# Scan stage of a recurrent mixer: which engine rounds two operands to their high parts, and in what order three engines and the matmul queue take their steps

## The reference, cut to what matters

```python
proj = jnp.einsum('bsd,od->bso', h, in_proj_w)
hBC = jax.nn.silu(causal_conv(hBC, conv_w, conv_b))
# hid: 128 heads x 64, B and C: 8 groups x 128, dt = softplus(...), A_full = A * dt
M = jnp.einsum('bcihn,bcjhn->bcijh', Ch, Bh) * jnp.transpose(L, (0, 2, 3, 4, 1))
Y_diag = jnp.einsum('bcijh,bcjhp->bcihp', M, hc)
decay_states = jnp.exp(A_cs[..., -1:] - A_cs)
states = jnp.einsum('bclhn,bhcl,bclhp->bchpn', Bh, decay_states, hc)
...
Y_off = jnp.einsum('bclhn,bchpn,bhcl->bclhp', Ch, prev_states, jnp.exp(A_cs))
yg = y * jax.nn.silu(gate)
ygr = ygr * jax.lax.rsqrt(jnp.mean(ygr * ygr, axis=-1, keepdims=True) + EPS)
out = jnp.einsum('bsd,od->bso', y, out_proj_w)
```

## Time and profile before

| | before |
|---|---|
| median of 3 runs | 1997.73 us |
| the profiled execution | 2001.5 us |
| its span, first to last instruction | 1999.6 us |
| PE busy | 1926.9 us (96%) |
| PEld busy | 1548.9 us (77%) |
| ACT busy | 1609.5 us (80%) |
| DVE busy | 1540.3 us (77%) |
| POOL busy | 1523.4 us (76%) |
| mean granted TensorE clock | 0.996 |

### The profile page before, as it was taken

The page is one execution under the profiler, slowest core; times in us unless marked ns, Lnnn a source line. Parts: engine busy times, 40 slices in busy tenths (PEclk is TensorE's granted clock), DMA queues, the critical chain, the costliest instruction groups (busy, mean ns, idle before and its releaser), DMA issues.

```text
span 1999.6 us, 32828 instructions
## 1 busy us (share of the span) xinstructions
PE 1926.9 (96%) x10675; PEld 1548.9 (77%) x10675; DVE 1540.3 (77%) x2806; ACT 1609.5 (80%) x3244; POOL 1523.4 (76%) x1114
## 2 busy tenths in 40 slices
PE   8999999999999999999999999999999999999998
PEld 6574667777888888888888878787878888888876
DVE  8787898866777777777777777777777878787878
ACT  5354866657898989898989898989888888888886
POOL 5644778647787878787878787878787787878887
PEclk9999999999999999999999999999999999999999
DMA  5625323543333333434333343434343434343333
GB/s 203 195 68 140 100 89 110 163 166 116 119 106 122 103 122 104 127 99 126 110 115 120 106 126 100 134 101 130 104 124 104 130 100 126 109 153 117 118 107 122
DMA packets 114474, 241.74 MB, mean 121 GB/s; under 512 B 23681, under 2 KB 24706, under 8 KB 113794
## 3 DMA queue, kind: packets, MB, share of 16 engines
q1 hardware_dynamic: 110466, 227.06, 36.7%
q0 software_dynamic: 3840, 12.59, 2.2%
HBM read 226.75 MB, written 12.85 MB: 120 GB/s over the span
## 4 chain that ended last, share of the span: by engine, by line
PE 28%; ACT 20%; DVE 13%; POOL 11%; issue 7%; DMA 1%; SPq 0%; ACTq 0%; DVEq 0%; POOLq 0%
PE ps L75 7%; PE ps L76 6%; PE ps L77 6%; POOL w_lo L2710 6%; ACT s_lm L2214 5%; PE ps L2129 4%; DVE s_cv L2457 3%; ACT s_scale L2237 3%; ACT s_cv L2247 2%; ACT s_hid L2281 2%; PE ps L2137 2%; POOL s_y_lo L2741 2%; DVE xs L2502 2%; POOL s_ssq L2720 2%; DVE s_hdt L2445 2%
## 5 line engine op out<-in xcount | busy, mean ns | idle before, releaser
L75 PE MATMUL ps<-h_hi,w_hi 128*128 128x512 f32 x1168 | 471.7, 404 | 13.5 <-POOL w_lo L2710 8.6
L2710 POOL TENSOR_TENSOR w_lo<-w_raw,w_hi 128x1024 fp32r<-128x1024 f32 x142 | 337.8, 2387 | 186.5 <-ACT w_hi L2197 186.5
L2457 DVE SCALAR_TENSOR_TENSOR s_cv<-ps,s_par,s_cv 128x511 f32<-128x511 f32 (+2 forms) x480 | 359.1, 748 | 128.3 <-ACT s_cv L2247 117.1
L76 PE MATMUL ps<-h_lo,w_hi 128*128 128x512 f32 x1168 | 456.0, 390 | 0.0
L77 PE MATMUL ps<-h_hi,w_lo 128*128 128x512 f32 x1152 | 450.9, 391 | 0.0
L2214 ACT ACTIVATE s_lm<-s_rows,s_steps 128x128 f32<-128x128 f32 x1024 | 324.0, 389 | 24.6 <-PE ps L2129 24.6
L2736 POOL TENSOR_TENSOR s_lm<-s_lm,s_cbt 128x512 f32<-128x512 f32 x256 | 327.8, 1307 | 14.4 <-ACT s_lm L2229 11.9
L75 PEld LDWEIGHTS ps<-h_hi,w_hi 128*128 128x128 f32 x1168 | 219.6, 188 | 68.1 <-DVE s_hid L2465 23.2
L77 PEld LDWEIGHTS ps<-h_hi,w_lo 128*128 128x128 f32 x1152 | 216.3, 188 | 47.1
L76 PEld LDWEIGHTS ps<-h_lo,w_hi 128*128 128x128 f32 x1168 | 220.1, 188 | 41.3 <-issue 0.2
L2741 POOL TENSOR_TENSOR s_y_lo<-s_hid,s_y_hi 128x512 fp32r<-128x512 f32 x120 | 155.7, 1298 | 66.4 <-ACT s_hid L2281 66.4
(11 more groups left out here) (338 smaller groups left out, 4464.6 us busy)
## 6 DMA issues: line engine op xcount, KB each, us to landing
w_raw<-in_w_in SPq DMA_DIRECT2D x144, 512.0 KB, 3.7
s_rows<-acs_dram SPq DMA_DIRECT2D x256, 256.0 KB, 3.6
s_wo_raw<-in_w_out SPq DMA_DIRECT2D x128, 256.0 KB, 3.2
w_raw<-in_gu_q SPq DMA_DIRECT2D x14, 512.0 KB, 3.6
f_d_q<-in_d_q SPq DMA_DIRECT2D x28, 256.0 KB, 2.7
f_d_w<-in_d_s SPq DMA_DIRECT2D x28, 256.0 KB, 3.7
table<-shifted SPq DMA_DIRECT2D x16, 256.0 KB, 2.6
xs<-in_x SPq DMA_DIRECT2D x8, 256.0 KB, 6.1
```

The lines of the kernel that those rows point to most:

```text
L75: nc.tensor.matmul(dst, l_hi, r_hi, start=start, stop=False)
L76: nc.tensor.matmul(dst, l_hi, r_lo, start=False, stop=False)
L2457: nc.vector.scalar_tensor_tensor(dst, src[:, 0:SEQ - d], par[:, v.b, 4 * j + 3 - d:4 * j + 4 - d], dst, ALU.mult, ALU.add).then_inc(conv_c ...
L2710: nc.gpsimd.tensor_tensor(w_lo[:, slot, :], w_raw[:, slot, :], w_hi[:, slot, :].bitcast(F32), ALU.subtract).then_inc(w_lo_ready, 1)
```

## The change

- **High parts on DVE.** `act_hdd` and `act_b` are gone. `dve_turn` makes `hdd_hi` itself, with a second multiplication of the same PSUM operand, between `hdd` and `hdt`; `dve_bt` copies the PSUM bank a second time, to `b_hi`, ahead of the copy to `b_l`. `dve_end` calls `dve_turn`, too, so the last unit makes six `hdd_hi` that nothing reads.
- **ACT's tail.** In doubles 0, 2 and 3 the tail was scale(a), scale(b), [rms in 3], the late weights, tanh(b). It is now scale(a), tanh(b), scale(b), the late weights, [rms in 3]. In double 1 tanh(b) goes ahead of the tap for C, and scale(a) behind that tap.
- **DVE.** In double 1 silu(b) goes ahead of the state steps. In doubles 0, 2 and 3 its order stays, with the state steps ahead of the convolution of b in double 0.
- **PE.** In double 2 OP_1(a) goes ahead of CB.
- **POOL.** In double 1 the rest of load 4 goes ahead of the sum of squares of b; `b_lo` goes behind the first `hdd_lo`.

```diff
--- before.py
+++ after.py
@@ -1700,11 +1700,12 @@
     if s == 1:
         jobs += [*both, one, two, (B_BANK, ("H", 1, B_AT))]
     else:
+        if s == 3:
+            jobs += [(A_BANK, ("SQ", 0, 0))]
+        jobs += [one]
         if s == 2:
             jobs += [(A_BANK, ("CB", 1, 0))]
-        if s == 3:
-            jobs += [(A_BANK, ("SQ", 0, 0))]
-        jobs += [one, *both, two]
+        jobs += [*both, two]
     return jobs + [(None, ("OP_1", 0, b)), (None, ("OP_2", 0, b))]
 
 
@@ -2215,14 +2216,6 @@
                                            bias=steps[:, v.b, 2, i, h:h + 1], scale=-1.0)
             ins.then_inc(diff_ready, 1)
 
-        def act_hdd(act, v, k):
-            act.wait_ge(took["T"], v.at(KC, k))
-            nc.scalar.activation(hdd_hi[:, :, k % 2, :], hdd[:, :, k % 2, :], ACT.Copy).then_inc(state_hi_ready, 1)
-
-        def act_b(act, v):
-            act.wait_ge(took["BT"], v.at(1, 0))
-            nc.scalar.activation(b_hi[:], b_l[:], ACT.Copy).then_inc(state_hi_ready, 1)
-
         def act_exps(act, v, k):
             for h in (2 * k, 2 * k + 1):
                 act.wait_ge(diff_ready, v.at(HG, h))
@@ -2323,9 +2316,6 @@
                     act_gate(act, v, k, bank(un, ("G", 1, k)))
                     act_exps(act, v, 0)
                     act_diff(act, v, 3, True)
-                    act_b(act, v)
-                    act_hdd(act, v, 0)
-                    act_hdd(act, v, 1)
             act_exps(act, v, 1)
             act_scale(act, v, 0, True)
             act_tap(act, *tile(KC - 1))
@@ -2355,36 +2345,33 @@
             if s == 1:
                 act_w(act, v, LOADS.index(("BC", 0)))
             act_exps(act, ua, a_on)
-            if s == 3:
-                act_b(act, v)
-            act_hdd(act, ua, a_on)
             act_gate(act, v, b, bank(un, ("G", 1, b)))
             if s:
                 act_tanh(act, v, tile_of(a), h_a)
-            act_hdd(act, ub, b_on)
             act_diff(act, ub, 2 * b_on)
             act_tap(act, v, tile_of(b), h_b)
             act_diff(act, ub, 2 * b_on + 1)
             if not s:
                 act_tanh(act, v, tile_of(a), h_a)
             act_exps(act, ub, b_on)
-            act_scale(act, ua, a_on)
             if s == 1:
                 c_bank, b_bank = bank(un, ("H", 1, C_AT)), bank(un, ("H", 1, B_AT))
+                act_tanh(act, v, tile_of(b), h_b)
                 act_tap(act, v, C_AT, c_bank)
-                act_tanh(act, v, tile_of(b), h_b)
+                act_scale(act, ua, a_on)
                 act_scale(act, ub, b_on)
                 act_w(act, *load_unit(un, LATE[s]))
                 act_tanh(act, v, C_AT, c_bank)
                 act_tap(act, v, B_AT, b_bank)
                 act_tanh(act, v, B_AT, b_bank)
                 return
+            act_scale(act, ua, a_on)
+            act_tanh(act, v, tile_of(b), h_b)
             act_scale(act, ub, b_on)
+            if load_unit(un, LATE[s]):
+                act_w(act, *load_unit(un, LATE[s]))
             if s == 3:
                 act_rms(act, un)
-            if load_unit(un, LATE[s]):
-                act_w(act, *load_unit(un, LATE[s]))
-            act_tanh(act, v, tile_of(b), h_b)
 
         def act_end(act, un):
             for k in range(KC):
@@ -2442,6 +2429,9 @@
             nc.vector.tensor_tensor(hdd[:, :, k % 2, :].rearrange("p c (h e) -> p c h e", h=2), by_head[:, 0:TB - 1],
                                     steps[:, v.b, 1, 0:TB - 1, pair].unsqueeze(3).to_broadcast((P, TB - 1, 2, HP)),
                                     ALU.mult)
+            nc.vector.tensor_tensor(hdd_hi[:, :, k % 2, :].rearrange("p c (h e) -> p c h e", h=2), by_head[:, 0:TB - 1],
+                                    steps[:, v.b, 1, 0:TB - 1, pair].unsqueeze(3).to_broadcast((P, TB - 1, 2, HP)),
+                                    ALU.mult).then_inc(state_hi_ready, 1)
             nc.vector.tensor_tensor(hdt[:, k % 2].rearrange("p c (h e) -> p c h e", h=2), by_head,
                                     steps[:, v.b, 0, :, pair].unsqueeze(3).to_broadcast((P, TB, 2, HP)),
                                     ALU.mult).then_inc(took["T"], 1)
@@ -2476,6 +2466,7 @@
 
         def dve_bt(dve, v, src):
             dve.wait_ge(done["BT"], v.at(1, 0))
+            nc.vector.tensor_copy(b_hi[:].rearrange("p c n -> p (c n)"), src[:, 0:3 * P]).then_inc(state_hi_ready, 1)
             nc.vector.tensor_copy(b_l[:].rearrange("p c n -> p (c n)"), src[:, 0:3 * P]).then_inc(took["BT"], 1)
 
         def dve_skip(dve, v):
@@ -2642,8 +2633,8 @@
             elif s == 1:
                 c_bank, b_bank = bank(un, ("H", 1, C_AT)), bank(un, ("H", 1, B_AT))
                 dve_tile(dve, v, tile_of(b), h[1])
+                dve_silu(dve, v, tile_of(b), h[1])
                 state()
-                dve_silu(dve, v, tile_of(b), h[1])
                 dve_skip(dve, v)
                 dve_tile(dve, v, C_AT, c_bank)
                 dve_silu(dve, v, C_AT, c_bank)
@@ -2720,13 +2711,19 @@
             nc.gpsimd.tensor_tensor(ssq[:], sq[:, 0, :] if k == 1 else ssq[:], sq[:, k % 2, :],
                                     ALU.add).then_inc(ssq_ready, 1)
 
+        def high_at(v, k):
+
+            split = ([0, 1, "b"] if v.first else [0, "b", 1]) + list(range(2, KC))
+            return v.at(KC + 1, split.index(k))
+
         def pool_hdd(pool, v, k):
-            pool.wait_ge(state_hi_ready, v.at(KC + 1, k + 1))
+            pool.wait_ge(state_hi_ready, high_at(v, k))
             nc.gpsimd.tensor_tensor(hdd_lo[:, :, k % 2, :], hdd[:, :, k % 2, :], hdd_hi[:, :, k % 2, :].bitcast(F32),
                                     ALU.subtract).then_inc(state_lo_ready, 1)
 
         def pool_b(pool, v):
-            pool.wait_ge(state_hi_ready, v.at(KC + 1, 0))
+            pool.wait_ge(state_hi_ready, high_at(v, "b"))
+            pool.wait_ge(took["BT"], v.at(1, 0))
             nc.gpsimd.tensor_tensor(b_lo[:], b_l[:], b_hi[:].bitcast(F32), ALU.subtract).then_inc(state_lo_ready, 1)
 
         def pool_m(pool, v, k):
@@ -2751,9 +2748,9 @@
             nc.gpsimd.memset(sum_eps[:], 256 * EPS)
             for c in range(2, NLOAD):
                 pool_w(pool, v, c)
-            pool_b(pool, v)
             pool_hdd(pool, v, 0)
             pool_hdd(pool, v, 1)
+            pool_b(pool, v)
             pool_m(pool, v, 0)
             pool_m(pool, v, 1)
             pool_w(pool, un.ahead(2), 0)
@@ -2767,12 +2764,12 @@
                 pool_sum(pool, un, a)
             pool_wo(pool, un, b)
             pool_y_lo(pool, un, b)
-            pool_sum(pool, un, b)
             if s == 1:
                 pool_w(pool, v, LOADS.index(("BC", 0)))
+            pool_sum(pool, un, b)
+            pool_hdd(pool, *pair_at(un, a + 2))
             if s == 3:
                 pool_b(pool, v)
-            pool_hdd(pool, *pair_at(un, a + 2))
             pool_hdd(pool, *pair_at(un, b + 2))
             pool_m(pool, *pair_at(un, a + 2))
             pool_m(pool, *pair_at(un, b + 2))
```

## The result

The changed kernel takes 2034.6 us (median of 4 runs, 2029.0 to 2039.5) against 1997.5 (4 runs, 1997.2 to 1998.4): a ratio of 1.0184, 95% interval 1.0152 to 1.0216. It is 37 us slower; 12 were forecast, and the measured median lies 1.6 us above the range. Its profiled execution has a span of 2029.2 us (2031.1 device time), 29.6 more than that of before.

The account below looks back on a forecast made before the run. PE was taken to bound the kernel, so any new PE wait is paid in full. Gains of 44 us and losses of 56 us made it 12 us slower: 1997.7 to 2010 us, range 1988 to 2033.

Parts of the forecast that it names:

- the clock's rival: PE's clock falls after double 1's new waits: 18 to 24 us more, 2028 to 2034, chance 0.18; not in the sum.
- if PE's clock is under 1 in it: Sign that the forecast is wrong: PE's granted clock below 1 in double 1.
- DIAG(b) of double 0: PE's wait at the start of double 0 for double 3's last silu goes: 18 us gained over 14 times.
- CB of double 2: OP_1(a), 1.4 us, covers PE's wait of 0.7 us for silu(a): 10 us gained over 15 units.
- Load 4: In double 1 its rest no longer stands behind a 1.25 us sum: 15 x 0.7 = 10 us gained.
- BT: In double 3 it takes the bank hdt frees, now behind hdd_hi: 15 x 0.47 = 7 us lost.
- The table load before gate(a): In double 0 the load makes gate(a) late for G(b): new PE wait 0.4 us, 14 times, 5.6 us lost.
- the rival of the drain: A drain of about 1.38 us on top of the table load: some 19 us more, 2029, chance 0.04.
- Double 1: Load 2's rest, queued behind the waiting tanh(b), comes late for G(a): 2.9 us, 14 times, 41 us lost.
- The first unit spared: It has no 2.9 us output step on DVE in double 0, so double 1's wait was counted 14 times.
- The last unit: Six hdd_hi on its DVE and PE loop cost 3 us; its start behind an earlier silu gains 1.5 us.
- the phase ahead of the units: ACT's three copies leave the path to the weights ahead of the 3.5 us hdd_lo wait: 1.2 us gained.

Follow-up runs that it names:

- e5_fill: The changed kernel plus 8 matmuls that nothing reads, issued on PE ahead of G(a) in double 1: 2025.8 us.
- e1: The changed kernel with ACT's tail of double 0 put back: scale(b) and late weights ahead of tanh(b): 1993.2 us, ratio 0.998.
- e6: The kernel before with the new orders, but ACT's old tail in double 0 and the high parts left on ScalarE: 1976.5 us, ratio 0.9893.
- e7: The kernel of e6 plus a one-column tanh on ACT ahead of y(a) in double 0, to place the table load there: 1971.4 us.
- e4: The changed kernel without the six hdd_hi of the last unit, which nothing reads: 2027.1 us, ratio 1.0151.
- e3: The kernel before with all the new orders, the high parts left on ScalarE: 2014.6 us, ratio 1.0087.
- e8: The kernel before with one step alone, tanh(b) ahead of scale(b) and the late weights in double 0: 2043.4 us, ratio 1.0232.

## Why the prediction was right or wrong

The direction held, and so did the place and the mechanism of the largest loss; the size was off by a factor of three, 12 against 37 us, and the time lies 1.6 us above the range, whose end had been put at 2033 though the clock's rival went to 2034. The step that failed first is the clock, which the sum had at nothing: PE's clock fell behind the new wait in 6 of 15 units, for 7.7 us. The prediction had named this itself as a sign of being wrong ("if PE's clock is under 1 in it"). In e5_fill, where it doesn't fall, the time is 2025.8 us, inside the range but still 16 above the forecast; the rest of the miss lies in terms that were mis-sized or left out, below. So it is luck that the time came out next to the rival of the clock, 2028 to 2034 with a chance of 0.18: that rival had all 14 units fall, for 18 to 24 us, on a sum that was itself too low.

- **DIAG(b) of double 0** (18 us off): right. DVE's wait of 4.4 us is gone, and so is PE's. The window of double 0 fell by 0.8 us with G(b)'s new wait in it; 0.9 had been forecast (22.3, measured 22.4).
- **CB of double 2** (10 us): right but for 0.2 us; the window is 23.1 and not 22.9.
- **Load 4** (10 us): its wait is gone, in e1 and e6 too, but these two show what comes instead, a wait for silu(a) of 0.8 and 0.4 us in the same place, which no step of mine had; in the changed kernel the wait for load 2 ahead of it leaves 0.1 of it. It is the largest omission in the working, though it costs the changed kernel almost nothing.
- **BT** (7 us): right. 0.39 us of idle time, 15 times, and double 3 at 23.2 as forecast. `hdd_hi` takes 548 ns, as its nearest row, `hdd`, had it (551).
- **The table load before gate(a)** (0.4 us, 14 times): right. 0.29 us of idle time and the overlap, 14 times; e7 moved the load and the wait went. The load is 1.28 us and the gate starts 0.02 behind it, in e6 at 1050.84 and 1052.14, so nothing is to be added on top of the load itself, and the rival of the drain did not come.
- **Double 1** (2.9 us, 14 times, 41 us): right in kind and nearly in size. DIAG(b) 0.5 and G(a) 2.3 us of idle time and twice the overlap make 3.0. Its window is 31.0, forecast 30.7.
- **The first unit spared**: wrong. Its wait is 2.3 us, too, and its double 1 takes 30.4. I took off 2.9 us for the output step that DVE does not have there. In its double 0 DVE stands idle at that place, for the transposition T(b):

```profile
474.39 0.56 DVE L2429 TENSOR_TENSOR s_hdd<-ps,s_steps 128x384 f32<-128x384 f32 x1 [2.60 <-PE ps L2077]
```

- **The last unit** (+3 - 1.5): the six `hdd_hi` cost 6.1 us, not 2.8. The missing term is mostly the collision of `y_lo` with POOL, 2.6 us; part of the rest may be the clock.
- **The clock** (0 us): this step failed most. I left it out of the likeliest case because the idle time was less than in both examples, and treated it as all or nothing. It is neither: 6 of 15 units in both profiles of the changed kernel, 5 in e4, 4 in e3, 10 in e8, at 1.2 to 1.4 us each, in e8 0.6.

For the profiled executions the difference is 29.6 us against 12. Without the 4.4 us by which the one before came late, it is 34.0, and the 22 us between forecast and result are: clock 8; first unit 3; the other units 0.6 us each beyond the sum of my parts, 8 to 9; last unit 4; less 1 for the phase ahead of the units, which gained 2.4 and not 1.2 (e1 and e4, with the same code there, gained 0.8). The median is 3.5 us above the profiled execution; what makes its two longer runs is open.

The sum of parts had also been added up less carefully than the windows: the windows named at its end give 1.0 us a unit, the measured ones 1.5, the parts 0.9.

Open: what else than the falls makes the two longer runs of the first set (2038 and 2039 us); what picks the units in which the clock falls; and what the new tails of doubles 1 and 2, silu(b) ahead of the state steps, the cover of CB and the place of load 4 are worth one by one, as none was run alone.

## What to carry to other kernels

When a queue is reordered so that an instruction comes "as early as it can", look at what stands behind it while it waits: here a tanh moved ahead of 2 us of ready work, and that work fed the weights of the next stage. Judge each reordering by double, stage or loop phase of its own: the same edit took away a wait of 1.2 us a unit at the end of double 3 and cost about 40 us in all at the end of double 0. And price a recurring wait of PE with the fall of the clock behind it, as a share of its occurrences and not as yes or no.

## What the runs showed of the hardware

- A wait of 0.5 and one of 2.3 us close behind it lowered PE's granted clock to 1.2 GHz in 6 of 15 units of the changed kernel and not in the others; each fall cost about 1.3 us. In e8_tail0_alone a wait of 2.3 us by itself did so in 10 of 15. The 1.2 us wait of the kernel before, 14 times, never did. Eight matmuls that nothing reads, put into the wait, ended the falls and made the kernel 6 to 9 us faster.
- 0.47 us more on DVE cost 1.0 us a turn in the last unit. Most of the excess came from an instruction with two SBUF inputs (1.04 us in the mean in e4_last, 1.37 in the changed kernel): it takes 0.75 us alone, and the rest of POOL's instruction and 0.55 us where one is under way.
- A tanh of one column, 1.28 us of table load and 0.1 to 0.2 of its own, can be used to place a table load in an idle stretch of ACT; it took 0.3 us off double 0, 14 times, 4 us here.
